# Head of a pre-norm attention-scan and mixture-of-experts kernel: the first token tile loaded in column halves, the last one normed by two engines

## The reference, cut to what matters

```python
def reference(L0_attn_x, L0_attn_w_qkva, L0_attn_gamma, L0_ffn_W1, ..., L0_ffn_Wg, L0_ffn_bg):
    # x: (8, 2048, 1024), w_qkva: (3072, 1024), W1: (8, 1024, 128), W2: (8, 128, 1024)
    def _L0_attn_ref(x, w_qkva, gamma):
        h = _rmsnorm(x, gamma)                      # x / |x| * sqrt(1024) * gamma
        q, kv, a = split(einsum('bnd,ed->bne', h, w_qkva), 3, axis=-1)
        a = sigmoid(a)
        y = scan over tokens of  y_t = a_t * y_(t-1) + kv_t
        return q * y
    def _L0_ffn_ref(x, W1, b1, W2, b2, Wg, bg):
        gate = softmax(x @ Wg + bg)                 # 8 experts, dense
        h = relu(einsum('bsd,edh->bseh', x, W1) + b1)
        y = einsum('bseh,eho->bseo', h, W2) + b2
        return einsum('bse,bseo->bso', gate, y)
    x = x + _L0_attn_ref(_layernorm(x), w_qkva, gamma)
    x = x + _L0_ffn_ref(_layernorm(x), W1, b1, W2, b2, Wg, bg)
```

## Time and profile before

| what | value |
|---|---|
| median of 3 runs | 324.69 us (324.61 to 324.82) |
| the profiled execution's own time | 325.49 us |
| its span, slowest core (core 7) | 323.9 us |
| spans of the cores 0 to 7 | 321.0, 323.2, 321.1, 323.5, 321.0, 322.9, 321.4, 323.9 us |
| PE, DVE, ACT, POOL busy on core 7 | 97%, 58%, 29%, 19% of the span |

### The profile page before, as it was taken

How to read it: one execution, slowest core, us unless ns; L and a number is a source line. 1 busy time by engine, 2 the same in 40 slices (tenths; PEclk the granted TensorE clock), 3 DMA queues, 4 the chain that set the end, 5 groups by cost and what they waited for, 6 DMA issues and landing times.

```text
span 323.9 us, 4976 instructions; the slowest of 8 cores (321.0 to 323.9 us)
## 1 busy us (share of the span) xinstructions
PE 313.2 (97%) x1602; PEld 141.6 (44%) x1602; DVE 187.8 (58%) x418; ACT 94.3 (29%) x147; POOL 62.2 (19%) x126
## 2 busy tenths in 40 slices
PE   7699999989999989999999999999999999999996
PEld 3245454454444434444444444444444444444443
DVE  0835387554778994363678784362778346733333
ACT  1472323573245214103236304104235320200000
POOL 4891003311311133001131322001131310000000
PEclk9989999999999999999999999999999999999999
DMA  6999999999993301966900401977000400164023
GB/s 133 206 158 177 220 207 197 223 177 212 207 219 66 132 2 28 168 216 186 274 39 1 131 18 29 170 222 225 10 0 2 144 3 0 51 143 200 0 116 143
DMA packets 21017, 40.93 MB, mean 126 GB/s; under 512 B 11424, under 2 KB 11840, under 8 KB 19968
## 3 DMA queue, kind: packets, MB, share of 16 engines
q1 hardware_dynamic: 16832, 25.87, 28.4%
q0 software_dynamic: 4160, 14.75, 24.9%
HBM read 40.25 MB, written 8.42 MB: 150 GB/s over the span
## 4 chain that ended last, share of the span: by engine, by line
PE 84%; DVE 7%; DMA 3%; issue 3%; ACT 1%; POOL 0%; SPq 0%; DVEq 0%; POOLq 0%; ACTq 0%
PE ps L653 44%; PE ps L743 17%; PE ps L762 17%; DMA xtok<-xt 3%; DVE sc L666 2%; PE ps L733 2%; PE ps L404 1%; PE ps L681 1%; DVE sc L675 1%; DVE bst L265 1%; ACT xn L297 1%; PE ps L710 1%; PE ps L418 1%; PE ps L492 0%; DVE bb L253 0%
## 5 line engine op out<-in xcount | busy, mean ns | idle before, releaser
L653 PE MATMUL ps<-pb,wq 128*128 128x512 bf16 x768 | 170.1, 379 | 0.6 <-DVE pb L524 0.6
L653 PEld LDWEIGHTS ps<-pb,wq 128*128 128x128 bf16 x768 | 74.2, 98 | 90.0 <-issue 4.8
L689 POOL TENSOR_TENSOR xb<-xb,sc 128x512 f32<-128x512 f32 x24 | 30.4, 1268 | 153.6 <-DVE sc L675 114.3
L743 PE MATMUL ps<-pb,w 128*128 128x512 bf16 x256 | 57.0, 380 | 0.0
L762 PE MATMUL ps<-h1g,w 128*128 128x512 bf16 x248 | 55.1, 380 | 0.0
L660 ACT ACTIVATE asig<-ps 128x512 f32<-128x512 f32 x32 | 19.0, 595 | 117.0 <-PE ps L653 98.2
L666 DVE TENSOR_TENSOR_SCAN sc<-asig,carry,ps 128x512 f32<-128x512 f32 x24 | 30.7, 1279 | 30.0 <-PE ps L653 16.6
L765 DVE TENSOR_TENSOR xb<-ps,xb 128x512 f32<-128x512 f32 x31 | 21.4, 691 | 29.6 <-PE ps L762 29.6
L743 PEld LDWEIGHTS ps<-pb,w 128*128 128x128 bf16 x256 | 24.3, 98 | 30.1 <-issue 2.2
L746 DVE SCALAR_TENSOR_TENSOR h1g<-ps,grep 128x512 bf16<-128x512 f32 x32 | 22.1, 692 | 25.9 <-PE ps L743 25.7
L762 PEld LDWEIGHTS ps<-h1g,w 128*128 128x128 bf16 x248 | 23.5, 98 | 29.2 <-issue 2.0
(11 more groups left out here) (118 smaller groups left out, 172.3 us busy)
## 6 DMA issues: line engine op xcount, KB each, us to landing
xtok<-xt SPq DMA_DIRECT2D x12, 512.0 KB, 10.2
outd<-xb SPq DMA_DIRECT2D x12, 512.0 KB, 4.1
grep<-gscr SPq DMA_DIRECT2D x4, 1024.0 KB, 5.7
xb<-xd SPq DMA_DIRECT2D x8, 512.0 KB, 6.0
wq<-wqd POOLq DMA_DIRECT2D x12, 256.0 KB, 35.3
wq<-wqd POOLq DMA_DIRECT2D x4, 768.0 KB, 21.2
w<-xt POOLq DMA_DIRECT2D x4, 512.0 KB, 32.6
xb<-xd POOLq DMA_DIRECT2D x4, 512.0 KB, 49.3
```

The costliest lines, as they stand in the source:

```text
L653: mm[i] = PE.do(lambda e, k=k: e.matmul(ps[banks[i]][:], wq[:, j, i, k, :], hbc[:, k, :], start=(k == 0), stop=(k == KC - 1)), h[k] if j = ...
L689: x2 = POOL.do(lambda e: e.tensor_tensor(xc[:, j, :], xc[:, j, :], sc[s][:], ALU.add), at, x_t[c][j])
L743: t = PE.do(lambda e, k=k: e.matmul(ps[b][:], w1[:, e_, k, :], xbf_of[c][:, k, :], start=False, stop=(k == KC - 1)), C[c]["xbf"][k] if e_ ...
```

## The change

Three edits, all in the head.

1. The first token tile is loaded by two DMAs of 256 KB, one per half of the columns, each with its own semaphore channel; each `bn_stats` of the tile waits for its half alone. SP has one more DMA to issue ahead of tile 1.
2. The last token tile is normed in two instructions of 512 columns, the first half by ACT, the second by DVE. The transposes of k < 4 wait for the first, the others for the second.
3. The turned tile of k = 7 goes to a bank of its own (`ps[2]`) and is copied by DVE; DVE copies k = 0, 2, 4, 6, 7 and ACT k = 1, 3, 5; the copy of k = 5 waits for its own transposes. Besides, 28 matmuls on the memset tile stand at the start in place of 32.

```diff
-        load_x0(0)
+        x00 = [SP.dma(lambda e, h=h: e.dma_start(
+            out=xtok[:, 0, h * TC:(h + 1) * TC], in_=xt[0, :, h * TC:(h + 1) * TC]), ch)
+            for h, ch in ((0, chan("d_xt0h")), (1, xt_ch[0]))]
+        xt_t[0].append(x00[1])
         load_x0(1)
...
                 t = DVE.do(lambda e, h=h: e.bn_stats(
-                    bst[:, i, h, :], tok_of[c][:, i, h * TC:(h + 1) * TC]), xt_t[c][i])
+                    bst[:, i, h, :], tok_of[c][:, i, h * TC:(h + 1) * TC]),
+                    x00[h] if c == 0 and i == 0 else xt_t[c][i])
...
-        turn_bank = [psT, psR[0], psR[1], ps[4]]
+        turn_bank = [psT, psR[0], psR[1], ps[4], ps[2]]
+
+        def turn_at(k):
+
+            return (turn_bank[4], 0) if k == KC - 1 else (turn_bank[k // 4 * 2 + k % 2], k % 4 // 2)
...
-                    C[0]["xn"][i], ms["identb"], tick=(i == NT - 1 or k == KC - 1))
+                    C[0]["xn"][i] if k < 4 or i < NT - 1 else last_half, ms["identb"], tick=(i == NT - 1 or k == KC - 1))
...
-        idle_mm(32)
+        idle_mm(28)
...
-        head_norm(3)
+        quick_r(0, 3, 4)
+        C[0]["xn"][3] = ACT.do(lambda e: e.activation(xn[:, 3, 0:TC], xtok[:, 3, 0:TC], AF.Identity,
+                                                      bias=nb1[:, 3:4], scale=r1[:, 3:4]), C[0]["r1"])
+        last_half = DVE.do(lambda e: e.tensor_scalar(xn[:, 3, TC:2 * TC], xtok[:, 3, TC:2 * TC], r1[:, 3:4], nb1[:, 3:4],
+                                                     ALU.mult, ALU.add), C[0]["r1"])
...
-            if k % 2 == 0:
+            if k % 2 == 0 or k == KC - 1:
                 C[0]["h"][k] = DVE.do(lambda e, k=k, src=src: e.tensor_scalar_mul(h_of[0][:, k, :], src, gam[:, k:k + 1]),
-                                      C[0]["turn"][k | 2], gam_t)
+                                      C[0]["turn"][k if k in (5, 7) else k | 2], gam_t)
...
-        st["psT"], psR_free[0], psR_free[1], ring_free[4] = [C[0]["h"][k] for k in (2, 3, 6, 7)]
+        st["psT"], psR_free[0], psR_free[1], ring_free[4], ring_free[2] = [
+            C[0]["h"][k] for k in (2, 3, 6, 5, 7)]
```

More of the change, by code:

```diff
@@ L490, in head_turn @@
             for k in (0, 2, 1, 3, 4, 6, 5, 7):
-                off = (k % 4 // 2) * TC + i * 128
-                t = PE.do(lambda e, k=k, off=off: e.matmul(
-                    turn_bank[k // 4 * 2 + k % 2][:].bitcast(BF16)[:, off:off + 128], xn[:, i, k * 128:(k + 1) * 128],
+                bank, half = turn_at(k)
+                off = half * TC + i * 128
+                t = PE.do(lambda e, k=k, off=off, bank=bank: e.matmul(
+                    bank[:].bitcast(BF16)[:, off:off + 128], xn[:, i, k * 128:(k + 1) * 128],
                     identb[:], start=True, stop=True, is_transpose=True),
-                    C[0]["xn"][i], ms["identb"], tick=(i == NT - 1 or k == KC - 1))
+                    C[0]["xn"][i] if k < 4 or i < NT - 1 else last_half, ms["identb"], tick=(i == NT - 1 or k == KC - 1))
                 if i == NT - 1:
@@ L517, in build_program @@
         head_stats(3, (1,))
-        head_norm(3)
+        quick_r(0, 3, 4)
[3 more added lines that the diff above has]
+                                                     ALU.mult, ALU.add), C[0]["r1"])
         head_turn(3)
         for k in range(KC):
-            off = (k % 4 // 2) * TC
-            src = turn_bank[k // 4 * 2 + k % 2][:].bitcast(BF16)[:, off:off + TC]
-            if k % 2 == 0:
+            bank, half = turn_at(k)
+            src = bank[:].bitcast(BF16)[:, half * TC:(half + 1) * TC]
+            if k % 2 == 0 or k == KC - 1:
                 C[0]["h"][k] = DVE.do(lambda e, k=k, src=src: e.tensor_scalar_mul(h_of[0][:, k, :], src, gam[:, k:k + 1]),
-                                      C[0]["turn"][k | 2], gam_t)
+                                      C[0]["turn"][k if k in (5, 7) else k | 2], gam_t)
             else:
```

## The result

The changed kernel takes 325.69 us (median of 7 runs) against 324.61 for the kernel before beside it. The ratio is 1.0036, with a 95% interval of 1.0026 to 1.0045: slower by 1.1 to 1.2 us (0.8 to 1.5 by the interval). The forecast was 324.6 us, no change, with a range up to 325.3. It was wrong in direction, and the time lies outside the range. It lies 0.1 us from the price of the rival that was given 10%, "the weights come later" (325.6).

The account below looks back on a forecast made before the run. The slowest odd core was taken to wait for chunk 1's token tile landing at 52.0 us. Head savings of 0.05 + 0.62 + 0.15 = 0.82 us were given back there, net 0: 324.6 us, range 323.6 to 325.3.

Parts of the forecast that it names:

- the weights come later: Rival, 10%: GpSimd's weight loads, gated by token tile 1, start 0.45 to 1.65 us later and delay later landings; 325.6 us.
- The way the kernel is bound: Chunk 1's first matmul comes 17.75 us after the later of first matmul plus 30.6 us or its token tile's landing.
- Between 0 and 1.2 I take 0, since the bytes and the queue stay the same.: Tile 0's load in 2 KB rows: cost taken as 0; rows moving at half the rate would cost 1.2 us.
- The extra issue: SP's additional DMA issue puts tile 1 and later loads about 0.45 us later into the queue; cost taken as nothing.
- The halves' gain of 0.59 us: Tile 0's statistics: 0.59 us saved if its first half lands at least 0.6 us earlier; about 0.05 left on core 7.
- The norm in halves: Last token tile's norm split between ACT and DVE: ACT's 1.24 us becomes 0.62, saving 0.62 us on all cores.
- The copies: Turned-tile copies in the head, shared anew between ACT and DVE: the k = 7 turn comes earlier, saving 0.15 us.
- "I take 0" for what the head saves on the slowest core: Core 7's head saves 0.82 us, but the token tile landing at 52.0 us gives it all back: net 0.
- some 0.6 us of waiting: Wait for chunk 1's token tile left in an ordinary run: profiled 1.39 us idle set against a median 0.80 us shorter.
- the first rival: Rival, 28%: the tile lands early enough on odd cores in ordinary runs, so the head's saving shortens the time; 323.7 us.
- The idle matmuls: Four fewer before the first turn: no path saving; a lower clock could add 0.4 us to transposes, taken as 0.
- The fit weighed in the prediction: Skill's transfer cost, 2.0 us fixed plus bytes over 436 GB/s: two halves 2.0 us dearer, 326.6 us; trace spoke against it.

Follow-up runs that it names:

- The version with tile 0 whole: The changed kernel with the first token tile loaded whole again, norm and copies edits and 28 idle matmuls kept: 324.15 us, ratio 0.9989.
- the 64-partition transfers: The kernel before with tile 0 loaded by two DMAs of 64 partitions each, rows of 4 KB: 325.31 us, ratio 1.0022.

## Why the prediction was wrong

**The way the kernel is bound: right.** The first matmul of chunk 1 stands 17.75 us behind the statistics of its tile 2 in every profile, and these come after the later of the head and the landing. The landing on a core that waits for it stands 40 to 42.5 us behind GpSimd's first weight issue in all these kernels. That is a band of 2 us, so it follows the issue, but not to the tenth.

**The failed step: "Between 0 and 1.2 I take 0, since the bytes and the queue stay the same."** This is the term on the rows of 2 KB. The bytes do stay the same, the rate at which they move does not: with the column halves the pair moved half as much between 4 and 6 us, tile 0 was complete 1.17 us later, and tile 1, the gate of the weights, behind it. The upper bound of 1.2 us, worked out for rows that move at half the rate, was the value: the first weights came 1.23 us later with the halves alone, and the time was 1.25 us longer. That both figures meet the bound so closely is in part luck, since the time is known to 0.4 us either way, and since the length of the rows alone brought only half of the delay and the second transfer the other half. The same mistake stands in the argument against the rival: tiles 2 and 3 in the queue "keep the engines at work, which only swaps the order of bytes". They were at work, share 0.76 to 0.98, and moved half. The rival's price of 1.0 us was near the result; its reason, one issue more and shorter rows, was right in the rows only.

**The extra issue: right at nothing** (+0.05 us; the interval of 0.999 to 1.001 is 0.3 us either way).

**The halves' gain of 0.59 us: right that the statistics could start early, wrong that the second half would be in time.** The first half started them at 5.96 us on core 5, and the second was waited for until 8.52, 0.68 us later than a whole tile had needed on core 7. Nothing was gained on that core. The forecast's condition, a first half at least 0.6 us ahead of the second, held on every core but did not help, since it was the second half that came late.

**The norm in halves: 0.42 in place of 0.62 us.** ACT's half took 0.81 us (a full norm 1.24), not the 0.62 of the 128x512 instruction of the earlier trace rows, which is a copy without scale and bias; that this makes the difference is argued. DVE's half took 0.55 to 0.58, between the bounds of 0.43 and 0.69, and was hidden.

**The copies: right.** 0.15 us, which comes behind the first matmul: 48.33 less 48.18 us to chunk 1. ACT's three end at 20.52 (18.68 + 1.84), DVE's five at 20.76.

**"I take 0" for what the head saves on the slowest core: too low.** The version with tile 0 whole saves 0.42 + 0.15 = 0.57 us in the head, and 0.38 of it (0.10 to 0.65 by the interval) arrives. I had put some 0.6 us of waiting into an ordinary run; most likely it was less, and the first rival ("the gain arrives") is the better account of these two edits.

**The idle matmuls: right at nothing for the time.** TensorE waited longer (2.88 us ahead of the first turn on core 5, 2.22 on core 7 before), the granted clock was 0.50 in the stretch from 13 to 14 us on cores 0, 2, 4, 5 and 7, which is 1.2 GHz, and eight turns took 1.01 to 1.06 us at that clock against 0.61. In the profile of the kernel before core 7 alone fell to 0.50, from 15 to 18 us. On cores 2 and 4 of the changed kernel, where three of the four turns ran at the lower clock, the head from the statistics of the late half to the first matmul took 11.4 to 11.5 us in place of 10.9. With 32 idle matmuls the time stayed (325.55 against 325.69).

```profile
12.67 1.01 PE L501 MATMUL ps<-identb,xn 128*128 128x128 bf16 x8 [2.88 <-ACT identb L514]
16.62 0.61 PE L501 MATMUL ps<-identb,xn 128*128 128x128 bf16 x8 [0.21 <-ACT sd L481]
```

The measured parts add up: +1.25 (halves) - 0.38 (norm and copies) = +0.87, and with the 0.2 us of the pause +1.05, against +1.08 measured. Each part is known to 0.3 or 0.4 us only, so the close sum is in part luck. That the pause supplies the last 0.2 is argued, not shown, since moving it off the path did not shorten the time.

The fit weighed in the prediction stands in the Trainium skill (DMA: Bandwidth & Descriptors, Anatomy of one DMA — SWDGE (gpsimd) path), for transfers that GpSimd issues; the token tiles of the head are issued by SyncE. Its fixed 2.0 us per transfer would have given 326.6 us, an estimate. Its direction was right where mine was wrong; as a price of 2.0 us for each further transfer it does not hold here, since an extra small transfer cost 0.05 us (0.3 either way). The Trainium skill (DMA: Bandwidth & Descriptors, Specifications) has transfers at line rate from 512 bytes on, so rows of 2 KB would be as good as 4 KB; the run with pieces of 2 KB in one transfer (tile 0 there 0.64 us later, pair at 817 against 931) does not agree, at least while both cores of a pair start their loads together.

**Left open:** why two transfers of 2 KB rows halve the rate of the pair when one such transfer takes only an eighth off it, and two transfers of 4 KB rows a sixth. The rows of a half lie 16 KB apart in memory and those of the one transfer next to each other two by two, and no run here separates that from the number of transfers. Nor does the start of the weights alone account for the 0.78 us of the 64-partition transfers.

## What to carry to other kernels

Ask of a split load not when its first part is there, but who waits for the load behind it: here GpSimd's wait for tile 1 held a stream of transfers, and the landing of a token tile in it sets the time 40 us later. Price that gate first, and take the upper bound of a term seriously where a stream hangs on it. If a load is to be split all the same, move the gate to something that still lands at its old time: with that, the column halves cost nothing (324.37 us), though they gained nothing either.

## What the runs showed of the hardware

The pair of cores moved half as much from 4 to 6 us with the tile in column halves, with the DMA engines nearly as busy as before (a mean share of 0.91 over the eight cores, against 0.99). From 6 to 7 us the rates are near each other again, 450 GB/s for a pair against 494. Which core of a pair is the late one is not fixed: it was the odd one in each pair of one profile of the kernel before, and core 0, 2, 5 and 6 in that of the changed kernel.

VectorE pauses for 0.46 to 0.49 us with nothing waited for, at the same instruction on all eight cores: at L253 before (164.79 us on core 7), at `w1b` once the stream is longer by a few instructions (107.88 us on core 5 in the changed kernel, 107.21 on core 1 with five memsets added), and at neither with the column halves alone. Its cause was not tried.

An ACT norm with scale and bias per partition of 128x512 took 0.81 us, two thirds of the 1.24 us of 128x1024, not half.
